# Ends of the score blocks rearranged: softmax sums inside the quantisation of the hidden row, exponentials and gates moved up, the last down product in another bank, every third quad summed in block 1

## The reference

```python
txt_proj = einsum('btd,de->bte', ctx, Ws); feat_proj = einsum('bfd,de->bfe', layernorm(x), W)
h = tanh(txt_proj[:, None] + feat_proj[:, :, None] + b)          # 2 x 2048 x 77 x 512
att = softmax(einsum('bftd,d->bft', h, w) + mask, axis=-1)
txt_h = einsum('bft,btd->bfd', att, ctx)
x = x + tanh(txt_h @ Wcw.T + bcw) * layernorm(x) + tanh(txt_h @ Wcb.T + bcb)
y = layernorm(x)                                                 # then, with q = FP4 round trip:
x = x + q(silu(q(y) @ q(w_gate).T) * (q(y) @ q(w_up).T)) @ q(w_down).T
```

## Time and profile before

| | us |
|---|---|
| three runs | 1612.20, 1609.06, 1609.72 (median 1609.72) |
| the profiled execution | 1610.59 |
| its span, first to last instruction | 1608.8 |
| PE busy / ACT busy / DVE busy | 1451.9 (90%) / 1360.1 (85%) / 1204.8 (75%) |
| tanh L561 / summed tanh L556 | 1007.4 in 956 / 242.3 in 67 |
| sums L880 | 183.7 in 268 |
| mean granted TensorE clock | 0.979 |

### The profile page before, as it was taken

The page is one execution under the profiler, slowest core; times in us unless marked ns, Lnnn a source line. Parts: engine busy times, 40 slices in busy tenths (PEclk is TensorE's granted clock), DMA queues, the critical chain, the costliest instruction groups (busy, mean ns, idle before and its releaser), DMA issues.

```text
span 1608.8 us, 24357 instructions
## 1 busy us (share of the span) xinstructions
PE 1451.9 (90%) x9752; PEld 640.4 (40%) x9752; DVE 1204.8 (75%) x1971; ACT 1360.1 (85%) x1238; POOL 246.4 (15%) x406
## 2 busy tenths in 40 slices
PE   6988888856898999988999999989999999879997
PEld 3334444412333333333343433433433343445554
DVE  6599998755676655677887677768877777899885
ACT  5999999999999999998899999998999998123331
POOL 1122222210111101111111111101111111112220
PEclk9999999988999999999999999999999999989999
DMA  4133332330021111110111111111211112123332
GB/s 139 40 86 80 85 79 71 90 63 7 8 50 21 31 39 30 35 38 14 39 39 38 39 39 39 39 25 39 45 37 34 38 39 39 38 59 69 75 69 56
DMA packets 180790, 77.91 MB, mean 48 GB/s; under 512 B 163883, under 2 KB 163883, under 8 KB 180677
## 3 DMA queue, kind: packets, MB, share of 16 engines
q1 hardware_dynamic: 179984, 75.00, 20.6%
q10 hardware_dynamic: 693, 1.36, 0.3%
HBM read 27.85 MB, written 8.39 MB: 23 GB/s over the span
## 4 chain that ended last, share of the span: by engine, by line
PE 59%; ACT 28%; DVE 11%; DMA 1%; issue 1%; POOL 0%; SPq 0%; ACTq 0%; DVEq 0%; POOLq 0%
PE rho L716 22%; ACT hring L561 21%; PE dn L805 10%; ACT hring L556 5%; PE gu0g L793 5%; PE gu1g L793 5%; PE gu1u L793 4%; PE gu0u L793 4%; PE gu1g L743 1%; PE gu1u L743 1%; PE gu0u L743 1%; PE gu0g L743 1%; DVE work L911 1%; DVE featT L880 1%; DVE work L925 1%
## 5 line engine op out<-in xcount | busy, mean ns | idle before, releaser
L561 ACT ACTIVATE hring<-featT,bias 128x1024 f32<-128x1024 f32 x956 | 1007.4, 1143 | 33.0 <-PE rho L716 33.0
L716 PE MATMUL rho<-hring,wslide 128*32 128x512 f32 x4928 | 601.5, 612 | 109.7 <-ACT hring L561 105.3
L716 PEld LDWEIGHTS rho<-hring,wslide 128*32 128x32 f32 x4928 | 133.9, 110 | 460.7 <-issue 241.2
L556 ACT ACTIVATE hring<-featT 128x4096 f32<-128x4096 f32 x67 | 242.3, 3617 | 8.7 <-DVE featT L880 5.2
L805 PE MATMUL dn<-wd_room,turned 128*128 128x512 f16 x1023 | 235.2, 382 | 0.0
L463 POOL TENSOR_SCALAR split_t<-sm 128x88 f32<-128x88 f32 (+2 forms) x91 | 22.4, 246 | 1206.9 <-DVE sm L902 1206.8
L880 DVE TENSOR_SCALAR featT<-featT,bias 128x1024 f32<-128x1024 f32 x268 | 183.7, 749 | 2.4
L1168 DVE TENSOR_TENSOR work<-sg,gu1u 128x352 f32<-128x352 f32 x64 | 33.4, 521 | 181.1 <-ACT sg L581 180.8
L805 PEld LDWEIGHTS dn<-wd_room,turned 128*128 128x128 f16 x1023 | 95.6, 98 | 158.4 <-issue 55.1
L793 PE MATMUL gu0g<-wg,turned 128*128 128x352 f16 x768 | 127.6, 317 | 17.4 <-DMA turned<-xq 12.0
L793 PE MATMUL gu1g<-wg,turned 128*128 128x352 f16 x768 | 125.5, 313 | 0.0
(11 more groups left out here) (170 smaller groups left out, 1359.9 us busy)
## 6 DMA issues: line engine op xcount, KB each, us to landing
xt<-in_x SPq DMA_DIRECT2D x32, 256.0 KB, 2.9
out<-xt SPq DMA_DIRECT2D x32, 256.0 KB, 2.4
work<-in_x SPq DMA_DIRECT2D x10, 512.0 KB, 3.8
xt<-in_x SPq DMA_DIRECT2D x6, 512.0 KB, 3.8
xt<-in_L_ffn_w_gate SPq DMA_DIRECT2D x11, 256.0 KB, 2.7
xt<-in_L_ffn_w_up SPq DMA_DIRECT2D x11, 256.0 KB, 2.7
work<-in_L_ffn_w_down SPq DMA_DIRECT2D x2, 704.0 KB, 4.5
xt<-in_L_ffn_w_down SPq DMA_DIRECT2D x2, 704.0 KB, 4.3
```

Source lines behind the costliest of these rows:

```text
L556: act.activation(hring[:, s // 2, :, 0:rows], featT[:, :, r:r + rows], ACT.Tanh).then_inc(tanh_ready, GRP)
L561: act.activation(hring[:, s // 2, g, (s % 2) * 512:(s % 2) * 512 + rows], featT[:, e, ROW0[k]:ROW0[k] + rows], ACT.Tanh, bias=bias[:, e, b ...
L716: last = pe.matmul(rho[SLOTW * g:SLOTW * g + SLOTW, hf * 512:hf * 512 + 512], wslide[:, e, SLOTW - 1 - r:2 * SLOTW - 1 - r], hring[:, s // ...
```

## The change

Five things, on three engines:

1. `GAP[1]` goes from 4 to 3. In block 1 the summed quads were 89, 93, ... 153 (17); now they are 89, 92, ... 152 (22). Blocks 2 and 3 keep their 25 each.
2. The exponentials of a block end stand at the end of tile 6 (14, 22), behind one tanh quad, and no longer ahead of the next tile's first Silu.
3. The sums of the softmax stand inside `quantise_hidden(6)`, between its big multiply and the mask, and no longer after `hidden(7, 1)`; `rows_tile(8)` takes the place they leave.
4. The gates stand ahead of the Silu of gate 0 of tile 7, the factors right after `hidden(7, 0)`.
5. The last down product goes into bank gu0g. It waits for `gu_drained[0]` (the last `hidden` on that bank) in place of `down_free` (the `result` of tile 30).

```diff
-GAP = {1: 4, 2: 3, 3: 3}
+GAP = {1: 3, 2: 3, 3: 3}
@@ scalar
                     if t - 1 in SOFTMAX_AT and n == 0:
-                        softmax_exp(SOFTMAX_AT[t - 1])
+                        softmax_gates(SOFTMAX_AT[t - 1])
                     silu_gate(t, n)
-                    if t - 1 in SOFTMAX_AT and n == 2:
-                        softmax_gates(SOFTMAX_AT[t - 1])
...
+                if t in SOFTMAX_AT:
+                    if issued < QUADS:
+                        tanh_quad(issued)
+                        issued += 1
+                    softmax_exp(SOFTMAX_AT[t])
@@ tensor
-            pe.wait_ge(down_free, NT - 1)
+            pe.wait_ge(gu_drained[0], 2 * NT)
...
-                        last = pe.matmul(dn[:, :], last_T[i][:, x, c - a // P, :], wd[:, y, c, :],
+                        last = pe.matmul(gu[0][0][:, :], last_T[i][:, x, c - a // P, :], wd[:, y, c, :],
@@ vector, quantise(..., between=None)
                     signal(ins, *read)
+                if between is not None:
+                    between()
                 if at is not None:
                     sum_quads(at)
@@ vector, result
-                signal(stt(row, dn[:, :], 1.0 / (W_PRE * H_PRE), row, ALU.mult, ALU.add), down_free, t + 1)
+                total = dn if t + 1 < NT else gu[0][0]
+                signal(stt(row, total[:, :], 1.0 / (W_PRE * H_PRE), row, ALU.mult, ALU.add), down_free, t + 1)
@@ vector, the loop over tiles
                 hidden(t, 0)
+                if ending is not None:
+                    softmax_factors(ending)
                 hidden(t, 1)
-                if ending is not None:
-                    softmax_sums(ending)
-                elif t + 1 < NT:
+                if t + 1 < NT:
                     rows_tile(t + 1)
                     sum_quads(before[t, 1] + 1)
...
-                if ending is not None:
-                    softmax_factors(ending)
-                    rows_tile(t + 1)
-                if t + 1 < NT:
+                if begun is not None:
+                    quantise_hidden(t, between=lambda: softmax_sums(begun))
+                elif t + 1 < NT:
                     quantise_hidden(t)
```

More of the change, by code:

```diff
@@ L882, in sum_quads, with quantise @@
                     sums[0] += 1
-            def quantise(src, n, hi, lo, m, least, pre, read=None, straight=None, at=None):
+            def quantise(src, n, hi, lo, m, least, pre, read=None, straight=None, at=None, between=None):
                 nb = n // QB
@@ L1169, in hidden, with quantise_hidden @@
                 sum_quads(before[t, n])
-            def quantise_hidden(t):
+            def quantise_hidden(t, between=None):
                 lift = W_PRE
@@ L1176, in quantise_hidden @@
                 signal(quantise(hbuf, INNER, hq[:, 0, :], hq[:, 1, :], hbuf, SCALE_MIN * lift, H_PRE / lift,
-                                straight=straight, at=before[t, 4]), hq_ready, t + 1)
+                                straight=straight, at=before[t, 4], between=between), hq_ready, t + 1)
                 sum_quads(before[t, 5])
```

## The result

| | before | changed |
|---|---|---|
| runs beside each other, median | 1610.82 us (1609.06 to 1612.2) | 1596.03 us (1594.65, 1594.80, 1597.27, 1597.56) |
| ratio, 95% interval | 1 | 0.9909 [0.9892, 0.9926] |
| the profiled execution, its span | 1610.59, 1608.8 | 1594.65, 1592.8 |
| PE / ACT / DVE busy | 1451.9 / 1360.1 / 1204.8 | 1448.8 / 1356.7 / 1218.2 |

The forecast was 1591 us for the median and 1591.8 for the profiled execution. The changed kernel is 0.9% faster, inside the range of 1584 to 1602; the size forecast, 1.2%, is a little more than came.

A forecast was written before the change was run, and what follows sets the result against it. ACT alone was taken to bound block 1, PE and ACT both to be near the bound in block 2. +0.3 - 10.2 - 7.3 - 0.4 - 1.2 = -18.8 us brought the span to 1590.0; forecast 1591 us, range 1584 to 1602.

The forecast's parts named there:

- Block 1: 400 to 690 us: five more summed quads save 3.3 us, quad 116's late sum costs 3.6, so +0.3 us.
- First block end: Around tiles 7 and 8: earlier exponentials, sums, gates and row remove PE's waits and half-speed matmuls, -10.2 us.
- the sum for quad 162: At the first block end: DVE's sum still comes before ACT needs it, but loses half of its lead.
- Half clock gone there: Sign at the first block end: PE's matmuls no longer run at half speed; 1.72 + 0.85 us of slow matmuls won.
- no gap of PE over 2.5 us: Sign in tile 7: PE's wait of 3.67 us for a quad disappears and none over 2.5 us remains.
- Second block end: Same steps one block later, with PE the later engine: its waits and slow matmuls shrink, -7.3 us.
- Third block end: No quads left and DVE is the chain: only its wait of 0.42 us goes, -0.4 us.
- Last product: End of program: 15 matmuls run early, a 4.7 us gap opens, the other 18 start at half speed, -1.2 us.
- (a): Rival at the block ends: only part of them pays, -9.7 us there, so 1599 us; chance 0.17.
- (b): Rival: block 1's gain comes whole and the last product runs at full clock, 1585 us; chance 0.09.
- (c): Rival at the block ends: exponentials come late and DVE stands inside the quantisation, about 1608 us; chance 0.07.
- (d): Rival in block 1: sums late all over, 3.6 us of ACT each, eight give 1616 us; chance 0.05.

The follow-up runs named there:

- experiment 2: Changed kernel with DVE allowed to sum quad 116 one place earlier; ratio 0.9864 to the kernel before, median 1588.96 us.
- experiment 6: Changed kernel with quad 116 summed earlier and 22 unused matmuls in the last gap, ratio 0.9859; then also 5 and 9 matmuls at the block ends, 0.9853.
- 2 and 5 together: Changed kernel with quad 116 summed one place earlier and 22 unused matmuls between the last product's two parts; ratio 0.9859, median 1586.76 us.
- experiment 4: Changed kernel with `rows_tile(8)` (16, 24) back behind `hidden(7, 3)`, the rest staying moved; ratio 0.9952 to the kernel before.
- experiment 3: Changed kernel with the exponentials back at the head of tile 7 (15, 23), just ahead of the gates; ratio 1.0002 to the kernel before.
- block 1 alone: Kernel before with only `GAP[1]` set from 4 to 3; ratio 1.0000 to the kernel before.
- last product alone: Kernel before with only the last down product moved to bank gu0g; ratio 0.9996 to the kernel before.
- experiment 5: Changed kernel with 22 unused matmuls between the 15 and the 18 of the last down product; ratio 0.9892 to the kernel before.
- experiment 7: The changed kernel run once more, unchanged, beside the kernel before (also called the repeat); ratio 0.9912.
- block ends alone: Changed kernel with `GAP[1]` back at 4, yet still with the moved last product; ratio 0.9886 to the kernel before.

## Why the prediction came out as it did

**Block 1: right in both halves, and the number with some luck.** +0.07 measured for +0.3. The late sum was predicted at quad 116 with 3.6 us; it is there with 3.52, and experiment 2 takes it away alone and wins 3.67. Quad 98, late by 0.6, was not foreseen: the count by places gave every other sum a lead of 0.6 or more. Tile 2 starts 0.65 late and tile 3 is level again. The luck is in the clock, for which the sum had no term: in three of the six profiles with the late sum it fell behind quad 116's gaps, and there the block cost +1.6 to +1.7.

**First block end: right in mechanism, 2.1 less than forecast** (-8.1 for -10.2). The steps hold: exponentials at 702.45 in a stretch where ACT waited before; the gates' wait 1.28; the gap of 3.67 and the slow matmuls behind it gone. Three details do not. Tile 8 was to begin 8 us earlier against tile 7's start and began 5.5 earlier; tile 9 was to begin 10 earlier and began 8.1 earlier. The clock fell during the quad at 727.34, where it had not before, which costs 1.4 of position: the same end gave -9.45 in the runs in which it did not fall there (experiments 2 and 6); the 0.7 that is left to the forecast was not traced. And the sum for quad 162, said to lose half of its lead, came 0.47 late: DVE's big multiply, from which the prediction counted on, ended 1.0 us later against tile 7's start than before (708.24 to 710.94, for 705.48 to 709.18). "Half clock gone there" was wrong; no gap of PE over 2.5 us, with 2.24 the longest in tile 7, was right.

**Second block end: 1.9 more than forecast** (-9.2 for -7.3). The sum had the slow matmuls at 1081 but left out those that stood before at 1064.44 and 1067.31, 1.02 and 0.64 us longer than usual. They were absent after. With a clock fall there it gave -7.86 (experiment 2, and 2 and 5 together), 0.6 from the forecast; in the kernel of experiment 6 in which the clock fell at neither end it gave -9.19. So the two misses of the block ends are for the most part one: the fall of the clock behind the pair of gaps 1.2 and 2.2 stood at the second end before and at the first end after. Together the ends gave -17.3 for -17.5.

**Third block end: right.** -0.37 for -0.4. PE's waits of 10.05 and 2.93 us for DVE there agree with DVE being the chain, and so does experiment 4, where two waits of DVE in that stretch and the later row cost 6.9, a fall of the clock included.

**Last product: a term of the sum that was mis-sized**, -0.10 measured for -1.2. The order of things was as told: 15 matmuls at full speed, a gap (5.08 for 4.7), then 18 slow ones. The prediction set the 18 at 18 x 0.22 + half of the slow time, 5.4 to 6.7 us, and 6.1 was taken. Here the slow time was 5.6 us (1582.74 to 1588.39, where the clock came back), which gives 3.96 + 2.8 = 6.8, the upper bound; and the row landed 3.8 after its quantisation, where 3.5 was taken. These two, 0.7 and 0.3, make nearly all of the 1.1. The slow time is not the same in every execution. In the kernel with quad 116's sum earlier (experiment 2) the 18 took

```profile
1579.17 5.63 PE L840 MATMUL gu0g<-wd_room,hring 128*128 128x512 f16 x18 [5.09 <-DMA hring<-work]
```

behind the same gap, and the stretch from tile 31 to the end gave -1.29; in experiment 3 it gave -1.51; in the five other profiles of this last product without matmuls in the gap, -0.10 to +0.08. The mean of the seven is -0.4, and the old product, too, differs by 0.7 between its two profiles (before, and block 1 alone). So the -0.10 is one draw, and the forecast of -1.2 lies within what single executions gave; on the mean the move is worth about nothing, as the ratio 0.9996 of the last product alone says. The rule of the Trainium skill that was weighed there ("TensorE: Matmul & The Clock Gate", "HAM oscillation — how this bites in real kernels") holds at this gap: a gap of 5.08 us, 18 matmuls at 0.38 us, and 0.23 without the gap (experiment 5). It does not decide at the gaps of 1.7 to 2.2 us, behind which the clock fell in some executions and not in others.

**The head**, which no term had: the profiled run began tile 0 1.7 us later than before. It is no effect of the change, since the same head gave 395.78 in the repeat; without it the span would have fallen by 17.7, and the forecast was 18.8. The profiled execution came 2.9 us above its forecast by this and the last product; the median came 5.0 above its own, since it also lies 1.4 above the profiled execution, where the forecast had put it 0.8 below.

**The rivals.** (a), only part of the block ends pays, 1599: refuted, since the ends pay 8.1 and 9.2 us where this rival gave them 9.7 together. Part of its condition did hold: half-speed matmuls came back behind another gap, and quad 162's sum came late by a hair. (b), 1585: its first half was a matter of one number (experiment 2), its second half needs PE busy in the gap (experiment 5); with both the kernel stands at 1586.8. (c), late exponentials: its condition did not hold, but its price, about 1608, is borne out by experiment 3 at 1609.7; an end cost 7.4 and 8.7 where 8.8 was set. (d), sums late all over block 1: two of 22 were late.

## What to carry to other kernels

When an engine's waiting time is to be filled, move both halves: the producer's instructions (here ACT's exponentials) into the wait of one engine, and the consumer's (DVE's sums) to where their input is then ready. Here the first two block ends win 17.3 us with the early exponentials and 1.2 without them. When a table of numbers decides how far one engine may run ahead of another, go through every entry with the times of the trace: one late sum of 22 took back all that five more summed quads gave, and the change would have been as good without that part. And where, as here, a last short piece of TensorE work stands behind a gap, unused matmuls in the gap can be worth more than starting the first half earlier.

## What the runs showed that was not expected

- The clock's falls are not a function of the code alone. In two executions of the changed kernel it stood at half from 86.5 to 93.4 us in one and from 81.5 to 84.9 in the other (experiment 7). Behind the same two gaps (1.87 and 2.23 us) in tile 3 the quad took 3.50 us in "block 1 alone" and 1.92 in the changed kernel; behind the pair 1.2 and 2.2 at the block ends it took 2.81 to 3.35 at one of the two and 1.92 at the other, in the kernel before, the changed one and that of experiment 2; behind 1.7 us in tile 6 it took 3.51 in "block ends alone" and 1.92 before. Each fall cost 1.3 to 1.7 us. What decides between them was not found; no run was made on it.
- Behind gaps of 3.8 to 3.9 us at the third end (1404 to 1405 us) the first gate product took 3.6 us in two kernels, and 1.96 behind a gap of 2.93 in the changed one. The longer gap goes with a shorter slow stretch at the gap of 10.05 us before it: in "block ends alone" the two products behind that gap took 3.50 and 1.95 us, in the changed kernel 3.70 and 2.65, so PE is done earlier and stands longer for the same DVE.
- The runs of the changed kernel stand 4.6 us apart in two groups (experiment 7). The start of tile 0, which varies by 3.7 us over all profiles, may be part of that; the upper group was not profiled.
